# Cross-attention scores from 96 stacked rows instead of three products of 32 rows

## The reference

```python
qp = q @ Wq.T                      # (8, 512, 512), 16 heads of 32
k, v = jnp.split(latent_kv @ Wkv_expand.T, 2, axis=-1)
scores = jnp.einsum('bhqd,bhkd->bhqk', qh, kh) * inv_sqrt_d
scores = jnp.where(causal, scores, jnp.finfo(scores.dtype).min)
attn = jax.nn.softmax(scores, axis=-1)
```

## Time and profile before

| what | value |
|---|---|
| median of 3 runs | 1795.61 us (1793.44 to 1797.07) |
| profiled execution | 1798.01 us, its span 1796.2 us |
| PE busy | 1435.2 us (80%) |
| DVE busy | 1178.7 us (66%) |
| ACT busy | 861.2 us (48%) |
| POOL busy | 547.4 us (30%) |
| mean granted clock of PE | 0.908 |
| DMA, mean over the span | 20 GB/s |

### The profile page before, as it was taken

How to read it: one execution, slowest core, us unless ns; L and a number is a source line. 1 busy time by engine, 2 the same in 40 slices (tenths; PEclk the granted TensorE clock), 3 DMA queues, 4 the chain that set the end, 5 groups by cost and what they waited for, 6 DMA issues and landing times.

```text
span 1796.2 us, 31869 instructions
## 1 busy us (share of the span) xinstructions
PE 1435.2 (80%) x11616; PEld 874.5 (49%) x11616; DVE 1178.7 (66%) x2539; ACT 861.2 (48%) x2098; POOL 547.4 (30%) x494
## 2 busy tenths in 40 slices
PE   1224899789988899889988899879988899789987
PEld 0113565446634565446644565446644565446633
DVE  8993455865578555865577556865578555865576
ACT  2442454455635554455635554455635554455522
POOL 5871000640046101640046101640046100640045
PEclk9999899998999899898998799897999899998998
DMA  5311000010000001010000000010000000000001
GB/s 181 112 46 36 1 1 25 7 25 1 2 24 13 18 1 24 7 24 1 2 24 13 18 2 24 7 24 1 2 24 13 18 1 25 7 19 1 2 1 24
DMA packets 25287, 36.10 MB, mean 20 GB/s; under 512 B 2480, under 2 KB 10672, under 8 KB 25136
## 3 DMA queue, kind: packets, MB, share of 16 engines
q1 hardware_dynamic: 25136, 34.09, 7.1%
HBM read 25.69 MB, written 8.39 MB: 19 GB/s over the span
## 4 chain that ended last, share of the span: by engine, by line
PE 43%; DVE 29%; ACT 9%; issue 9%; POOL 2%; DMA 0%; SPq 0%; ACTq 0%; DVEq 0%; POOLq 0%
PE psum L526 9%; PE psum L1110 7%; PE psum L1127 7%; PE psum L1148 5%; DVE top L820 5%; PE psum L1164 4%; DVE inter L846 3%; DVE nmx L770 3%; PE psum L1187 3%; PE psum L1209 2%; PE psum L1113 2%; DVE q L816 2%; ACT silu L1007 2%; DVE pt L783 2%; PE psum L1136 2%
## 5 line engine op out<-in xcount | busy, mean ns | idle before, releaser
L503 POOL TENSOR_TENSOR rstd<-var_eps,minus_half 128x1 f32<-128x1 f32 x96 | 59.8, 623 | 894.9 <-DVE var_eps L497 894.9
L969 ACT ACTIVATE p<-psum,nmx 128x384 f32<-128x384 f32 (+3 forms) x512 | 265.8, 526 | 68.4 <-DVE nmx L770 64.0
L770 DVE TENSOR_REDUCE nmx<-psum 128x2 f32<-128x256 f32 (+3 forms) x256 | 210.7, 823 | 114.6 <-PE psum L1113 114.6
L783 DVE COPY pt<-psum 128x128 f32<-128x128 f32 (+3 forms) x256 | 124.6, 487 | 193.9 <-PE psum L1127 193.5
L1127 PE MATMUL psum<-ident,p 128*128 128x128 f32 x1280 | 206.4, 289 | 21.1 <-ACT pt L993 18.1
L1110 PE MATMUL psum<-k_hl,q_hl 32*128 32x128 f32 (+3 forms) x1536 | 204.3, 373 | 16.4 <-DVE q_hl L757 11.7
L691 POOL TENSOR_TENSOR inter<-inter,rscale 128x512 f32<-128x512 f32 x128 | 141.3, 1104 | 209.8 <-DVE rscale L854 209.2
L1209 PE MATMUL psum<-wd_sb,iq_t 128*128 128x512 bf16 x512 | 147.6, 415 | 37.8 <-DVE x_res L863 28.1
L993 ACT COPY pt<-psum 128x128 f32<-128x128 f32 (+3 forms) x256 | 109.3, 427 | 141.6 <-PE psum L1127 140.2
L1127 PEld LDWEIGHTS psum<-ident,p 128*128 128x128 f32 x1280 | 143.8, 146 | 56.0 <-ACT pt L993 26.6
L1187 PE MATMUL psum<-wg_sb,xq_t 128*128 128x512 bf16 x512 | 148.9, 418 | 26.2 <-ACT xq_t L1000 21.7
(11 more groups left out here) (104 smaller groups left out, 2397.5 us busy)
## 6 DMA issues: line engine op xcount, KB each, us to landing
x_in<-in_x_dram SPq DMA_DIRECT2D x32, 256.0 KB, 4.1
out_dram<-x_res SPq DMA_DIRECT2D x64, 128.0 KB, 2.4
w_raw<-in_w_gate_dram SPq DMA_DIRECT2D x16, 256.0 KB, 2.8
w_raw<-in_w_up_dram SPq DMA_DIRECT2D x16, 256.0 KB, 3.2
w_raw<-in_w_down_dram SPq DMA_DIRECT2D x16, 256.0 KB, 3.8
ctx_in<-in_ctx_t_dram SPq DMA_DIRECT2D x8, 256.0 KB, 2.9
wq_raw<-in_wq_t_dram SPq DMA_DIRECT2D x1, 1024.0 KB, 8.0
wo_sb<-in_wo_t_dram SPq DMA_DIRECT2D x1, 1024.0 KB, 10.2
```

The costliest lines, as they stand in the source:

```text
L770: dve.tensor_reduce(nmx2[:, u % UNITS, 2 * pr:2 * pr + 2], where(("scores2", oc, qt, pr))[:, :, 0:(qt + 1) * P], AX_X, ALU.max, negate=Tru ...
L783: free(dve.tensor_copy(pt2[:, hh, 0:m], where(label)[:, 0, 0:m]), label)
L969: ins = act.activation(p2[:, (4 * u + hh) % P2_RING, 0:m], where(label)[:, hh % 2, 0:m], ACT.Exp, bias=nmx2[:, u % UNITS, hh:hh + 1], accu ...
```

## The change

The high and low parts of K and Q now go to `k_s` and `q_s`, one buffer each. From there SP copies them by DMA into `k_st` and `q_st`, two buffers each by the parity of the group, so that for each head three blocks of 32 rows stand below each other: high, low, high of K and high, high, low of Q. One product over 96 rows then gives what three products over 32 rows gave. For K and for Q a group needs 4 heads x 3 blocks = 12 DMAs, each of 32 partitions by 2 KB. The units qt 0 and 1 of a batch's first group (`direct`) still take the three products, from `k_s` and `q_s`.

Q's projection is now done in the unit qt 1 instead of qt 2. Its split and K's split move with it to qt 1 on both engines. For the later three groups of a batch K's projection stays at its place on PE but goes to bank C0, between the transposes of qt 0 and those of qt 1. SP's moves stand in front of the load of the next context, and in the last step of a batch in front of the last store of the batch. The other hunks move buffers in SBUF.

```diff
 def psum_plan:
-            plan["TO"[oc % 2]].append(("k", oc))
+            if oc % OC == 0:
+                plan["T"].append(("k", oc))
             plan["TO"[oc % 2]] += [("q", oc), ("outT", oc)]
...
+                if qt == 0 and oc % OC + 1 < OC:
+                    plan["C0"].append(("k", oc + 1))
...
+        def direct(oc, qt):
+            return oc % OC == 0 and qt < 2
 SP:
+                def spread_heads(stacks, split, parts, oc):
+                    for pr in range(2):
+                        for j in range(2):
+                            rows = slice((2 * pr + j) * HD, (2 * pr + j + 1) * HD)
+                            for g, i in enumerate(parts):
+                                ins = sp.dma_start(stacks[oc % 2][pr][g * HD:(g + 1) * HD, j, :].bitcast(F32),
+                                                   split[rows, i, :].bitcast(F32))
+                                yield ins
+                def move_k(oc):
+                    until_freed(sp, ("k", oc))
+                    if oc >= 2:
+                        until_filled(sp, ("scores2", oc - 2, T - 1, 1))
+                    for ins in spread_heads(k_st, k_s, (0, 1, 0), oc):
+                        ins.then_inc(S["k_moved"], 16)
+                def move_q(oc):
+                    until_freed(sp, ("q", oc))
...
+                    for ins in spread_heads(q_st, q_s, (0, 0, 1), oc):
+                        ins.then_inc(S["q_moved"], 16)
+                move_k(0)
+                move_q(0)
                 for b in range(B):
+                    for oc in range(b * OC + 1, (b + 1) * OC):
+                        move_k(oc)
+                        move_q(oc)
                     if b + 1 < B:
                         sp.wait_ge(S["ctx_ready"], b + 1)
...
                     for t in range(T):
+                        if t == T - 1 and b + 1 < B:
+                            move_k((b + 1) * OC)
+                            move_q((b + 1) * OC)
                         until_freed(sp, ("down", b * T + t))
 DVE, head, i == 17 (was 18):
+                        low_k(b * OC)
 DVE, unit:
                             maxima(u + 1, 0)
+                        if qt == 1 and more:
+                            low_k(oc + 1)
                         take_probs(u, 0)
                         if qt == 0 and oc % OC:
                             take_out(oc - 1)
-                        if qt == 1 and more:
-                            low_k(oc + 1)
-                        if qt == 2 and more:
-                            low_q(oc + 1)
                         if u + 1 < end:
                             maxima(u + 1, 1)
+                        if qt == 1 and more:
+                            low_q(oc + 1)
 ACT, high_k (high_q alike):
-                    if oc >= 2:
-                        until_filled(act, ("scores2", oc - 2, T - 1, 1))
+                    if (oc - 1) % OC == 0:
+                        until_filled(act, ("scores2", oc - 1, 1, 1))
+                    if oc:
+                        act.wait_ge(S["k_moved"], MOVED * oc)
 ACT, unit:
+                        if qt == 1 and more:
+                            high_k(oc + 1)
                         if u + 1 < end:
                             exps(u + 1, 0)
+                        take_probs(u, 0)
                         if qt == 1 and more:
-                            high_k(oc + 1)
-                        if qt == 2 and more:
                             high_q(oc + 1)
-                        take_probs(u, 0)
 PE, score2, if not direct(oc, qt):
+                        pe.wait_ge(S["k_moved"], MOVED * (oc + 1))
+                        pe.wait_ge(S["q_moved"], MOVED * (oc + 1))
                         for j in range(2):
+                            pe.matmul(where(label)[:, j, 0:m], q_st[oc % 2][pr][0:STACK, j, qt * P:(qt + 1) * P],
+                                      k_st[oc % 2][pr][0:STACK, j, 0:m], start=True, stop=False)
 PE, unit:
-                        if qt == 2 and more:
+                        if qt == 1 and more:
                             project_q(oc + 1)
```

More of the change, by code:

```diff
@@ L159, in decoder_layer @@
         shift2 = sb("shift2", [P, T])
-        xn1 = sb("xn1", [P, 2, D])
         tmp1 = sb("tmp1", [P, 2, D])
@@ L181, in decoder_layer @@
             ("wq_raw", [P, C, D], F32), ("wkv_raw", [P, 2 * D], F32))
-        k_hl, = phase(("k_hl", [P, 2, 2, N], F32R))
+        STACK = 3 * HD
+        MOVED = 4 * 3 * 16
+        k_st0, k_s, q_s, k_st1, q_st10 = phase(
+            ("k_st0", [P, 2, 2, N], F32R), ("k_s", [P, 2, N], F32R), ("q_s", [P, 2, N], F32R),
+            ("k_st1", [P, 2, 2, N], F32R), ("q_st10", [P, 2, N], F32R))
         inter = sb("inter", [P, RING, CH])
+        silu = sb("silu", [P, 2, CH])
         x_f = sb("x_f", [P, D])
-        silu = sb("silu", [P, 2, CH])
+        xq = sb("xq", [P, 2, D], BF16)
         q8 = sb("q8", [P, RING + 2, CH], FP8)
@@ L188, in decoder_layer @@
         iq_t = sb("iq_t", [P, RING, CH], BF16)
-        xq = sb("xq", [P, 2, D], BF16)
         xq_t = sb("xq_t", [P, 2, D], BF16)
@@ L193, in decoder_layer @@
         rscale = sb("rscale", [P, RING + 1, CH // BLOCK])
+        q_st0 = sb("q_st0", [P, 2, 2, N], F32R)
+        q_st11 = sb("q_st11", [P, 2, N], F32R)
         x_t2 = sb("x_t2", [P, 2, C, N], F32R)
-        q_hl = sb("q_hl", [P, 2, 2, N], F32R)
+        xn1, = phase(("xn1", [P, 2, D], F32))
         p2 = sb("p2", [P, P2_RING, N])
@@ L199, in decoder_layer @@
         v_sb = sb("v_sb", [P, T, D])
+        q_st = [[q_st0[:, 0], q_st0[:, 1]], [q_st10[:], q_st11[:]]]
+        k_st = [[k_st0[:, 0], k_st0[:, 1]], [k_st1[:, 0], k_st1[:, 1]]]
         psum = es.enter_context(nc.psum_tensor("psum", [P, 8, 512], F32))
@@ L237, in decoder_layer @@
             "xt2_high",
-            "q_high", "k_high",
+            "q_high", "k_high", "q_moved", "k_moved",
             "nmx_ready", "p2_ready", "values_done", "rx_ready",
@@ L756, in low_q @@
                     dve.wait_ge(S["q_high"], oc + 1)
-                    free(dve.scalar_tensor_tensor(out=q_hl[:, oc % 2, 1, :], in0=where(label)[:, 0, :],
-                                                  scalar=SCALE, in1=q_hl[:, oc % 2, 0, :].bitcast(F32),
-                                                  op0=ALU.mult, op1=ALU.subtract), label)
+                    ins = dve.scalar_tensor_tensor(out=q_s[:, 1, :], in0=where(label)[:, 0, :], scalar=SCALE,
+                                                   in1=q_s[:, 0, :].bitcast(F32), op0=ALU.mult, op1=ALU.subtract)
+                    free(ins, label)
                 def low_k(oc):
@@ L763, in low_k @@
                     dve.wait_ge(S["k_high"], oc + 1)
-                    free(dve.tensor_tensor(k_hl[:, oc % 2, 1, :], where(label)[:, 0, :],
-                                           k_hl[:, oc % 2, 0, :].bitcast(F32), ALU.subtract), label)
+                    ins = dve.tensor_tensor(k_s[:, 1, :], where(label)[:, 0, :], k_s[:, 0, :].bitcast(F32), ALU.subtract)
+                    free(ins, label)
                 def maxima(u, pr):
@@ L869, in head @@
                         low_xt2(b * T + 1)
+                        low_k(b * OC)
                     if i == 18:
                         low_xt2(b * T + 2)
-                        low_k(b * OC)
                     if i == 19:
@@ L946, in high_q @@
                     until_filled(act, ("q", oc))
-                    if oc >= 2:
-                        until_filled(act, ("scores2", oc - 2, T - 1, 1))
-                    act.mul(q_hl[:, oc % 2, 0, :], where(("q", oc))[:, 0, :], SCALE).then_inc(S["q_high"], 1)
+                    if (oc - 1) % OC == 0:
+                        until_filled(act, ("scores2", oc - 1, 1, 1))
+                    if oc:
+                        act.wait_ge(S["q_moved"], MOVED * oc)
+                    act.mul(q_s[:, 0, :], where(("q", oc))[:, 0, :], SCALE).then_inc(S["q_high"], 1)
                 def high_k(oc):
-                    if oc >= 2:
-                        until_filled(act, ("scores2", oc - 2, T - 1, 1))
                     until_filled(act, ("k", oc))
-                    act.copy(k_hl[:, oc % 2, 0, :], where(("k", oc))[:, 0, :]).then_inc(S["k_high"], 1)
+                    if (oc - 1) % OC == 0:
+                        until_filled(act, ("scores2", oc - 1, 1, 1))
+                    if oc:
+                        act.wait_ge(S["k_moved"], MOVED * oc)
+                    act.copy(k_s[:, 0, :], where(("k", oc))[:, 0, :]).then_inc(S["k_high"], 1)
                 def exps(u, pr):
@@ L1101, in score2 @@
                     m = (qt + 1) * P
-                    if qt == 0 and pr == 0:
-                        until_freed(pe, ("k", oc))
-                        until_freed(pe, ("q", oc))
                     label = ("scores2", oc, qt, pr)
                     until_free(pe, label)
-                    for n, (i, k) in enumerate(((0, 0), (0, 1), (1, 0))):
+                    if direct(oc, qt):
```

(16 more changed lines are left out.)

2 lines of the change are left out of this document (added).

## The result

The changed kernel takes 1975.44 us (median of 4, 1971.38 to 1977.77) against 1794.53 us (1793.06 to 1797.07): 1.100 times as long, 95% interval 1.098 to 1.103. Its profiled span is 1974.1 us, 177.9 above that of before, 22.2 a batch. The forecast was 1931 us.

The account below looks back on a forecast made before the run. PE was taken as nearly full in cross-attention, then waiting for 24 DMA issues on one queue: 7.7 + 2 x 4.6 = 16.9 us a batch, 8 batches, +135 us, giving 1931 us; range 1790 to 1995.

Parts of the forecast that it names:

- the first wait: At unit 2 of a batch, PE reaches the first stacked product at 206.95, moves land at 211.2: 4.2 us wait.
- The new wait for C0: In the loop, project_k now needs bank C0, which DVE must free first: 0.83 us added.
- Rival A: SP's issues of 32 partitions take 0.33 us, PE hardly waits, kernel gets faster: 1757 us; chance 0.17.
- B's 0.43: SP's issues take 0.43 us each, leg 12.3 us, no change to speak of: 1801 us; chance 0.13.
- The issue: On SP's queue, each move's issue takes 0.57 us; 23 of them plus a 2.4 us landing make 15.5 us.
- C's 0.68: SP's issues take 0.68 us as for x, leg 18.0 us, slower still: 2011 us; chance 0.10.
- One sign of being wrong: Starts of successive groups, forecast 28 us apart; above 30 us, landing or the queue costs more than the issue.
- The clock in the loop: Behind PE's wait the clock falls to 0.50 for about 3 us, adding 1.3 us to the loop.
- The start: First group's low_k ends at 195.67; the next group's first score group starts at 229.8, 7.7 us late.
- The tail: In a batch's last group, PE's 1.8 us saving comes half through and the clock's fall costs about as much: 0.
- The saving of a stacked score group: On PE, two steps where there were three: 0.16 us saved at 128 columns, 0.24 at 384, 0.30 at 512.
- Q's earlier projection: In rival A's loop on PE, it covers the waits of qt 1, gaining back some of C0's 0.8 us.

Follow-up runs that it names:

- the order run: The kernel before with both projections and both splits in their new places, no moves, three products over 32 rows from double buffers: 1767.0 us, ratio 0.984.
- eight moves: All three terms in the order run's order, with 8 moves a group instead of 24, one product over 64 rows and one over 32 per head: 1790.9 us.
- both queues: The changed kernel with all 24 moves, heads 0 and 1 issued by SP, 2 and 3 by POOL, each pair with its own count: 1742.2 us.
- the same kernel with 64 rows: The kernel on both queues, stacked products reading the first 64 of 96 rows, third term left out, all 24 moves kept: 1783.5 us.

## Why the prediction was right, and where its sizes were off

The mechanism was as forecast, in each of its places: trains of issues on SP, PE's wait at their end, the clock's fall behind it. In the first batch the first wait was 4.5 us (4.2 forecast), ended by a DMA. low_k's end followed 3.0 us after it (3.1). The waits at the later groups were longer than the 5 to 6 us forecast, 6.4 to 9.4. The new wait for C0 was there (0.95 us in the changed kernel). The clock was at 0.50 behind each wait. Rival A's condition, an issue of 0.33, is false, and so is B's 0.43. The issue in a train, 0.63, lies just above the 0.46 to 0.62 to which I gave 0.60, on the way to C's 0.68, and so does the time: 1975 us is inside the range but above the 1850 to 1970 of the forecast itself. One sign of being wrong that I had named came up: successive groups started 29.5 to 31.9 us apart, 30.6 on average, where I said 28 and drew the line at 30. Of the reasons I gave for such a case, the landing is false (2.0 us, not 2.4) and the queue is true: with the gaps and with single issues of up to 1.9 us a train takes 0.63 an issue. The clock's longer fall is the other half.

What fell short is the size, 135 us for 178. Over the eight batches of the changed kernel's trace:
- **The issue**: 0.57 taken, 0.63 measured in a train. A leg, from the end of low_k to PE's start, was 16.6 to 18.0 us and 17.1 on average, not 15.5; the moves land sooner, but their issues take longer. There are four legs in a batch: 32 x 1.6 = 51 us. This is the mis-sized term that explains most of it.
- **The clock in the loop**: 1.3 us taken, from a fall of 3 us in the earlier trace rows. The part of the fall that came behind waits of 6.6 us and more was 6 us long. From the score group to K's projection 10.5 us (232.01 to 242.51) passed, 10.4 on average, not 9.2. That is 1.2 more for each of two loops, 19 us. K's projection to low_k's end took 3.1, not 3.4 (5 us back).
- **The start**: low_k of a batch's first group ended sooner than I took it (195.0 for 195.67 in the first batch), and so did some steps behind it. By difference, 7 us back.
- **The tail** gave back about 2 us a batch where I put 0: 15 us the other way.

So the errors add up to 70 us one way and 27 the other, and the number looks better by that than the terms were.

Two steps were wrong but hidden by the wait. The saving of a stacked score group: I had one step of three (0.24 us at 384 columns), and from transposes to transposes it is 1.37 - 0.91 = 0.46, because the changes of height go too. And Q's earlier projection, which I counted only as cover in rival A: the order run shows it with C0 as 1.6% faster, so rival A's 1757 was too slow a price for free moves; 1742 came out with moves not quite free, though on two queues.

The clock is also part of why savings on PE and times did not move one for one, though no run separates it. By its mean it stood at 0.50 for span x 2 x (1 - clock): 330 us before, 215 in the order run, 247 with eight moves, 222 with both queues and 307 in the same kernel with 64 rows. Which waits bring a fall stays open. In both_queues it stayed up behind the waits of 1.18 and 1.08 us (1.00 from 217 to 260), and behind the one of 2.12 it fell (0.57 from 261 to 265); the order run, with waits of 0.76 and 0.86 us in a group, kept it up where the kernel before, with 0.84 and 0.53, did not.

## What to carry to other kernels

Price a DMA that rearranges data on the chip by its issue on the queue, not by its bytes: count the issues between the last input and the first reader, multiply, add one landing, and compare with the time the reader leaves. If it is the train that is late, split it over queues by consumer and give each consumer its own count, before reducing bytes. And time a change's parts apart: here the order alone won 28 us, the stacks with their moves on one queue lost 208 against that, and with the same moves on two queues they won another 25.

## What the runs showed of the hardware

- An issue on SP with an SBUF source took 0.59 to 0.60 us, for 16 KB as for 256 KB; 64 KB from HBM took 0.42. POOL's issue of the same move took 0.50, and it landed after 2.3 instead of 2.0 us.
- Products over 96 rows ran beside transposes of full height without the cost of a change; over 64 rows the same instructions cost 0.29 us more for a score group of 384 columns, 1.20 us against 0.91.
- 24 moves of 64 KB in every 22 us, which nobody waited for, left the time (1765.0 against 1767.0 us) and the busy times of PE, DVE and ACT where they were.
- Behind a wait of PE of 6.6 us the granted clock was 0.50 for six more microseconds, and eight transposes took 1.97 us instead of 1.09.
